# An RWKV layer in fp32 on one core: reordered last steps, and idle matmuls in TensorE's first waits

## The chip, the cores and the metric

One Trainium2 chip, one NeuronCore. The metric is the device time of one execution in microseconds (us). TensorE (PE) multiplies, VectorE (DVE), ScalarE (ACT) and GpSimd (POOL) do the elementwise work, and SyncE (SP) issues the transfers.

## The reference

An RWKV block over 32 sequences of 128 tokens and 512 channels, all in fp32. Cut to its steps:

```python
xn = ln(x); sx = token_shift(xn, prev1)
xxx = tanh((xn + sx*maa_x) @ maa_w1)                 # five small mixtures
x5 = xn + sx * (maa_stack + xxx @ maa_w2)
w = exp(-exp(time_decay + tanh(x5[1] @ decay_w1) @ decay_w2))
k, v, r, g = x5[0] @ Wk.T, x5[2] @ Wv.T, x5[3] @ Wr.T, silu(x5[4] @ Wg.T)
# per head of 16 channels, over the tokens t:
#   out_t = r_t @ (u * k_t v_t + s);  s = k_t v_t + w_t * s
att = groupnorm(out) * gn_w + gn_b
x = x + (att * g) @ Wo.T
xn2 = ln(x); xk, xr = mix(xn2, token_shift(xn2, prev0))
x = x + sigmoid(xr @ Wr2.T) * (square(relu(xk @ Wk2.T)) @ Wv2.T)
```

## The kernel before, in words

A block is two sequences (b = 0, 1) and there are 16 blocks. The program is unrolled into steps -2 to 17, and step i holds, as a software pipeline, the first half of block i + 1 or i + 2 (layer norm `xT`, `h`, the mixtures `mixW` to `mixV`, `z`, `decay`, then the dense products `k`, `g`, `r`, `v`), the recurrence of block i, and the second half of block i - 1 (group norm, `yT`, `wo`, layer norm, `x2T`, `kk`, `rr`, `wv`). The steps -2 to 0 lack the later parts and have little work. Step 15 (`LAST`) lacks the first half; in it the second half of block 14 runs with a recurrence of block 15, and the second half of block 15 is done one sequence at a time, by the functions `tail` (names with `@0` or `@1`). What is left of it lies in step 16.

The order of the work on each engine is written out by hand in lists: `PE_ORDER`, `ACT_ORDER`, `DVE_ORDER`, `POOL_ORDER` and `SP_ORDER` for the steps before the last, and `PE_LAST` and its likes (lines 75 to 91) for the last two. Each engine does its list in order and waits at semaphores inside each item.

The recurrence of a block has 8 units n = 0 to 7, one for each sequence and each group of 128 channels. The names that matter for it:

- `chain1`, `chain1b` (VectorE, from line 539): products of decays, k and r; the late half `chain1b` releases most of what follows. `rch1`, `rch1b` (GpSimd, from line 402) do the same for r, and `rch1b` stands behind `yT` in GpSimd's list of the last step.
- `M0` to `M7` (`mask`, SyncE, line 309): 8 copies of 12 KB each from `rst` to one of two buffers `rm`. Mn waits until `levels` of unit n - 2 is done (`levels_done`) and for GpSimd's `rchain` of its sequence.
- `A0` to `A7` (`levels`, TensorE, line 1020): 64 short products from such a buffer into `at_ps`. `E0` to `E7` (`evict`, ScalarE, line 863) take them out.
- `V0` to `V7` (`read_out`, TensorE, line 1081): two products with the first state `s0` and with `kvs`, then 16 short ones that wait for the eviction. The first state is loaded by `S0` and `S1` (`load_s0`, line 319), one buffer for both sequences, so `S1` waits for V3 (`read_done`).
- `kt0`, `kv0`, `kt1`, `kv1` (`turn_k`, `outer`): the state between the two halves of a sequence; `aT0`, `aT1` (`turn_att`): turns the result of a sequence.

For the second half: `yT` on TensorE turns `cen` (line 1127, 8 transposes) when GpSimd's `gn_scale` (line 484) is done. ScalarE's `yT` (line 848) takes the result out, GpSimd's `yT` (line 489) multiplies it with the gate, and then `wo.0` and `wo.1` can start (line 1119, 8 instructions each). For sequence 0 of the last block the chain aT0, `att0`, `gn_sum@0`, `gn_sub@0`, `gn_square@0`, `gn_var@0`, `gn_std@0`, `gn_rec@0`, `gn_scale@0` leads to `yT@0`.

At the start TensorE waits for four small loads (`sel_in`, with `ident` among them) and for `setup`, which counts the memsets of GpSimd and VectorE. SyncE's list of step 0 has M1 and S0 behind M0 and the load of `x`. `columns` (line 1111) does the dense products: 32 instructions for a group such as `k`.

A matmul in fp32 is two instructions in the trace, a transpose is one.

Of the kernel before, what the change touches and what calls it, by code (L numbers as in the profile page):

```python
# [71 lines left out]
LAST = NBLK - 1  # L72
POST = ("gn_sum", "gn_sub", "gn_square", "gn_var", "gn_std", "gn_rec", "gn_scale", "yT", "wo", "ln2_stats",
        "ln2", "x2T", "kk", "rr", "wv")
PE_LAST = {LAST: ["kt0", "V7", "kv0", "wv.0", "aT1", "A0", "wv.1", "V0", "A1", "c02_1", "V1", "c1v_1", "A2", "V2",
                  "A3", "V3", "yT", "kt1", "wo.0", "kv1", "wo.1", "aT0", "A4", "V4", "yT@0", "A5", "V5", "x2T", "A6", "V6",
                  "wo@0", "A7", "V7+", "kk.0", "aT1+", "kk.1", "x2T@0", "rr.0", "rr.1", "kk@0", "yT@1", "rr@0"],
           LAST + 1: ["wv.0", "wo@1", "wv.1", "wv@0", "x2T@1", "kk@1", "rr@1", "wv@1"]}
ACT_LAST = {LAST: ["kt0", "dec0", "att1", "E0", "gn_square", "gn_std", "E1", "vtm1", "E2", "E3", "yT", "kt1", "dec1",
                   "att0", "E4", "gn_square@0", "gn_std@0", "E5", "yT@0", "x2T", "E6", "E7", "att1+", "kk",  # L80
                   "gn_square@1", "x2T@0", "gn_std@1", "rr", "kk@0", "yT@1", "rr@0"],
            LAST + 1: ["x2T@1", "kk@1", "rr@1"]}
# [4 lines left out]
POOL_LAST = {LAST: ["gn_sub", "rch1", "wv", "c02_1", "gn_scale", "bon1", "yT", "rch1b", "gn_sub@0", "gn_scale@0",  # L87
                    "ln2_stats", "yT@0", "ln2_stats@0", "gn_sub@1", "gn_scale@1", "yT@1"],
             LAST + 1: ["ln2_stats@1", "wv"]}
SP_LAST = {LAST: ["M1", "S0", "F1", "M2", "out", "x2", "x2@0", "x2@1", "M3", "M4", "M5", "S1", "M6", "M7"],  # L90
           LAST + 1: ["out", "out@0", "out@1"]}


class Block:
# [21 lines left out]
def build(nc, A):  # L116
    ctx = ExitStack()
    with ctx:
        def sb(name, shape, dt=F32):
            return ctx.enter_context(nc.sbuf_tensor(name, shape, dt))  # L120
# [11 lines left out]
        dec1 = sb("dec1", [P, G, DEC])  # L132
        vecs = sb("vecs", [P, 16, G])
        ident = sb("ident", [P, P])
# [47 lines left out]
        yT = sb("yT", [P, G, TB])  # L182
        sq = yT[:, :, :].rearrange("p g t -> p (g t)")
        prev0 = sb("prev0", [P, G, NB])
        x2 = sb("x2", [P, NB, E])
# [17 lines left out]
        att_ps = ctx.enter_context(nc.psum_tensor("att_ps", [P, 2, NB, G, 64], F32))  # L203
# [49 lines left out]
        def ran(name, step):  # L253
            blk = step + AHEAD[name]
            return 0 <= blk < NBLK and not (blk == LAST and name in POST)
# [27 lines left out]
        def units(step):  # L283
            return step >= 0 and step < NBLK
# [11 lines left out]
        def _(sp):  # L296
# [35 lines left out]
            def step(i, at_):  # L332
                for name in SP_LAST.get(i, SP_ORDER if i < LAST else []):
                    if "@" in name:
# [502 lines left out]
        def _(ac):  # L837
# [163 lines left out]
            def step(i, at_):  # L1001
                for name in ACT_LAST.get(i, ACT_ORDER if i < LAST else []):
                    if "@" in name:
                        tail(name[:-2], int(name[-1]))
                    elif name == "att1+":
                        stage("att1", i + 1, at_.plus(1))
                    elif name[0] == "E":
                        if units(i):
                            evict(at_, int(name[1:]))
                    elif ran(name, i):  # L1010
                        stage(name, i, at_)
# [4 lines left out]
        def _(pe):  # L1016
# [33 lines left out]
            def turn_k(at_, b):  # L1050

                pe.wait_ge(kchain, at_.count(2 * NK, NK * (b + 1)))
                if at_.past(2, b - 1):
                    pe.wait_ge(att_ready, at_.count(2, b - 1))
                if at_.past(2, b):
                    pe.wait_ge(kvs_ready, at_.count(2, b))
                for g in range(G):
                    last = pe.transpose(kv_ps[:, g * P:(g + 1) * P], k64[:, 64 * g:64 * g + P], ident[:, :])
                last.then_inc(kt_done, 1)

            def outer(at_, b):

                pe.wait_ge(kt_ready, at_.count(2, b + 1))
                pe.wait_ge(vtm_ready, at_.count(2, b + 1))
                for g in range(G):
                    v = bass.AP(vtm[b], g * 2 * P, [[2 * E, 64], [64, G], [48, 2], [1, S]])
                    last = pe.matmul(kv_ps[:, g * P:(g + 1) * P], kt[:, g * P:(g + 1) * P], v,  # L1067
                                     start=True, stop=True)
                last.then_inc(kv_done, 1)

            def turn_att(at_, b):

                pe.wait_ge(attT_ready, at_.count(2, b + 1))
                pe.wait_ge(kvs_ready, min(at_.count(2, b + 2), 2 * NBLK))
                if at_.past(2, b):
                    pe.wait_ge(att_ready, at_.count(2, b))
                for g in range(G):
                    last = pe.transpose(kv_ps[:, g * P:(g + 1) * P], bonv[:, b, g, :], ident[:, :])
                last.then_inc(aT_done, 1)

            def read_out(at_, n):

                b, g = n // G, n % G
                o = att_ps[:, :, b, g, :]
                if g == 0:
                    pe.wait_ge(kvs_ready, at_.count(2, b + 1))
                    pe.wait_ge(s0_in, at_.count(32, 16 * (b + 1)))
                    pe.wait_ge(rchain, at_.count(2 * NR, NR * (b + 1)))
                    if at_.past(2, b - 1):
                        pe.wait_ge(attT_ready, at_.count(2, b - 1))  # L1090
                pe.matmul(o[:, 0, :], s0[:, g, :], rst[:, b, g, R64A:RST], start=(g == 0), stop=False,
                          skip_group_check=True)
                pe.matmul(o[:, 1, :], kvs[b][:, g * P:(g + 1) * P], rst[:, b, g, R64B:R16C], start=(g == 0),
                          stop=False, skip_group_check=True)
                pe.wait_ge(at_ready, at_.count(UNITS, n + 1))
                for odd in range(2):
                    for quad in range(4):
                        h = 2 * quad + odd
                        first = (g * HG + h) * 32
                        for c in range(2):  # L1100
                            rows_ = slice(64 * c, 64 * c + 64)
                            last = pe.matmul(o[32 * quad:32 * quad + 32, c, :],  # L1102
                                             vtm[b][rows_, first:first + 32], at[rows_, h, :], start=False,
                                             stop=(g == G - 1), skip_group_check=True)
                last.then_inc(read_done, 1)
# [161 lines left out]
            def step(i, at_):  # L1267
                for item in PE_LAST.get(i, PE_ORDER if i < LAST else []):
                    name, _, part = item.partition(".")
                    if "@" in name:  # L1270
                        tail(name[:-2], int(name[-1]))
                    elif name == "V7+":
                        read_out(at_, 7)
                    elif name == "aT1+":
                        turn_att(at_, 1)
                    elif name == "V7":
                        if units(i - 1):
                            read_out(at_.plus(-1), 7)
                    elif name in ("kt0", "kt1"):
                        if units(i):  # L1280
                            turn_k(at_, int(name[2:]))
                    elif name in ("kv0", "kv1"):
                        if units(i):
                            outer(at_, int(name[2:]))
                    elif name in ("aT0", "aT1"):
                        if ran(name, i):
                            turn_att(at_.plus(AHEAD[name]), int(name[2:]))
                    elif name[0] == "A":
                        if units(i):
                            levels(at_, int(name[1:]))  # L1290
                    elif name[0] == "V":
                        if units(i):
                            read_out(at_, int(name[1:]))
                    elif ran(name, i):
                        stage(name, i, at_, int(part or 0))
            run(step)


# [43 lines left out]
```

## Time and profile before

| | us |
|---|---|
| median of 3 runs | 1679.78 |
| the three runs | 1679.78, 2635.2, 1679.77 |
| the profiled execution | 1679.46 |
| its span, first to last instruction | 1677.7 |
| TensorE busy (matmul) | 1572.8 (94%) |
| VectorE, GpSimd, ScalarE busy | 997.1, 623.9, 512.8 |

Times in the profile count from the first instruction. "Idle before" is the time that an engine stood still in front of a group, and the arrow names what ended it; "issue" is time in which nothing that the profile shows was waited for. The granted clock is the share of TensorE's full 2.4 GHz: 1.00, or 0.50 for 1.2 GHz. For the first 23 us no clock was recorded and the windows say 1.00.

### The profile page before, as it was taken

The numbers are of one execution on the slowest core, as the hardware profiler recorded it, in microseconds if no ns is written. First come the engines' busy times: TensorE is split into PE (matmuls) and PEld (weight loads), VectorE is DVE, ScalarE is ACT, GpSimd is POOL, SyncE is SP. The second block draws the span as 40 slices with busy tenths as digits, with TensorE's granted clock in tenths as the row PEclk, the third lists the DMA queues.
The fourth block names the chain that finished last, engine by engine and source line by source line (L and its number), as shares of the span: only waits on it lengthen the run. The fifth ranks groups of instructions, "written<-read, shape, count | busy, mean of one in ns | idle before, by whom it ended". The sixth has DMA issues, their size and how long they took to land.

```text
span 1677.7 us, 45471 instructions
## 1 busy us (share of the span) xinstructions
PE 1572.8 (94%) x19680; PEld 1178.2 (70%) x19680; DVE 997.1 (59%) x1990; ACT 512.8 (31%) x910; POOL 623.9 (37%) x512
## 2 busy tenths in 40 slices
PE   4869799999999999999999999999999999999788
PEld 3658577777767777776777777677777767777454
DVE  3255665767566566756656675665667666555442
ACT  1122333324232332423233232322323232232231
POOL 3133442525244253524325352432535243252311
PEclk8879899999999999999999999999999999999799
DMA  7010100102010010201001020201102020010200
GB/s 272 0 34 25 47 23 21 51 18 63 22 59 24 21 61 7 64 22 61 22 23 61 6 64 21 61 22 34 49 7 64 21 61 22 22 47 8 61 16 25
DMA packets 56423, 67.70 MB, mean 40 GB/s; under 512 B 23264, under 2 KB 40032, under 8 KB 55200
## 3 DMA queue, kind: packets, MB, share of 16 engines
q1 hardware_dynamic: 56224, 64.79, 12.3%
q8 instruction: 156, 2.56, 0.7%
q14 instruction: 43, 0.35, 0.1%
HBM read 43.75 MB, written 8.39 MB: 31 GB/s over the span
## 4 chain that ended last, share of the span: by engine, by line
PE 77%; DVE 13%; ACT 4%; POOL 2%; issue 2%; SPq 1%; DMA 1%; ACTq 0%; POOLq 0%; DVEq 0%
PE pair L1111 27%; PE pair L1119 19%; PE pair L1165 4%; PE at_ps L1045 4%; PE at_ps L1038 3%; PE pair L1189 2%; PE kv_ps L1067 2%; PE att_ps L1102 2%; DVE kT L585 2%; PE pair L1127 2%; DVE x L674 2%; PE pair L1191 2%; PE pair L1145 2%; POOL cen L477 2%; DVE gT L704 1%
## 5 line engine op out<-in xcount | busy, mean ns | idle before, releaser
L1111 PE MATMUL pair<-x,wts 128*128 128x256 f32 x2048 | 463.5, 385 | 16.5 <-ACT kT L859 15.2
L1111 PEld LDWEIGHTS pair<-x,wts 128*128 128x128 f32 x2048 | 386.9, 191 | 80.1 <-ACT kT L859 18.0
L451 POOL TENSOR_TENSOR x<-x,xnT 128x1024 f32<-128x1024 f32 x80 | 178.5, 2231 | 226.8 <-DVE x L674 226.1
L674 DVE SCALAR_TENSOR_TENSOR x<-pair,vecs,sx 128x256 f32<-128x256 f32 x320 | 132.4, 475 | 123.8 <-PE pair L1165 123.4
L868 ACT ACTIVATE at<-at_ps 128x512 f32<-128x512 f32 x128 | 76.2, 596 | 194.9 <-PE at_ps L1045 194.7
L1119 PE MATMUL pair<-wts,yT 128*128 128x512 f32 x240 | 112.3, 612 | 4.1 <-POOL yT L489 4.1
L1045 PE MATMUL at_ps<-rm,kc 128*16 128x128 f32 (+1 forms) x2048 | 112.5, 279 | 0.0
L1119 PE MATMUL pair<-wts,cen 128*128 128x512 f32 x240 | 110.8, 604 | 0.0
L1111 PE MATMUL pair<-yT,wts 128*128 128x256 f32 x480 | 107.8, 382 | 0.0
L1119 PE MATMUL pair<-wts,sx 128*128 128x512 f32 x240 | 107.0, 599 | 0.7 <-ACT cen L854 0.7
L1038 PEld LDWEIGHTS at_ps<-rm,kc 128*8 128x8 f32 (+5 forms) x6144 | 67.4, 97 | 49.0 <-issue 37.5
L1111 PEld LDWEIGHTS pair<-yT,wts 128*128 128x128 f32 x480 | 89.9, 190 | 14.4 <-issue 2.8
L1038 PE MATMUL at_ps<-rm,kc 128*8 128x32 f32 (+5 forms) x6144 | 83.7, 197 | 10.5 <-DMA rm<-rst 9.7
L462 POOL TENSOR_TENSOR bonv<-bonv,p 128x256 f32<-128x256 f32 x32 | 43.3, 1352 | 130.7 <-DVE p L690 130.7
L555 DVE SCALAR_TENSOR_TENSOR bonv<-rT,vecs,kT 128x128 f32<-128x128 f32 x128 | 36.5, 347 | 92.8 <-ACT rT L859 62.0
L1165 PE MATMUL pair<-h,maa 32*128 32x128 f32 x1024 | 78.1, 293 | 10.9 <-DVE gT L704 7.4
L472 POOL TENSOR_TENSOR bonv<-bonv,p 128x256 f32<-128x256 f32 x32 | 24.5, 767 | 170.0 <-DVE p L697 170.0
L1165 PEld LDWEIGHTS pair<-h,maa 32*128 32x128 f32 x1024 | 65.4, 194 | 22.8 <-DVE gT L704 11.9
L1119 PEld LDWEIGHTS pair<-wts,sx 128*128 128x128 f32 x240 | 44.4, 190 | 52.4 <-issue 50.2
L408 POOL TENSOR_TENSOR rT<-rT,t 128x256 f32<-128x256 f32 x32 | 36.8, 1148 | 117.6 <-DVE p L568 117.6
L1119 PEld LDWEIGHTS pair<-wts,yT 128*128 128x128 f32 x240 | 44.3, 194 | 50.8 <-issue 49.0
L1045 PEld LDWEIGHTS at_ps<-rm,kc 128*16 128x16 f32 (+1 forms) x2048 | 78.4, 105 | 0.6
(192 smaller groups left out, 2679.6 us busy)
## 6 DMA issues: line engine op xcount, KB each, us to landing
rm<-rst SPq DMA_DIRECT2D x1024, 12.0 KB, 1.8
xu<-in_x SPq DMA_DIRECT2D x16, 512.0 KB, 3.9
wts<-in_wts SPq DMA_DIRECT2D x8, 1024.0 KB, 14.1
kvs<-in_s SPq DMA_DIRECT2D x32, 256.0 KB, 3.0
s<-in_s SPq DMA_DIRECT2D x32, 256.0 KB, 2.9
x<-in_x SPq DMA_DIRECT2D x15, 512.0 KB, 4.8
out<-sx SPq DMA_DIRECT2D x15, 512.0 KB, 3.0
prev<-in_prev SPq DMA_DIRECT2D x32, 4.0 KB, 3.5
```

The source lines that it names most:

```text
L408: gp.tensor_tensor(leaf[:, :, 2:4], leaf[:, :, 2:4], t2[:, :].rearrange("p (f q) -> p f q", q=2)[:, :, 0:1] .broadcast_to([P, G * 32, 2]), ...
L451: gp.tensor_tensor(t, t, xnT[:, :, :, 1:L1].rearrange("p g b t -> p (g b) t"), ALU.add).then_inc(x5_ready, 1)
L462: gp.tensor_tensor(leaf[:, :, 2:4], leaf[:, :, 2:4], m2[:, :, :, 0], ALU.add)\
L477: gp.tensor_tensor(cen[:, :, :].rearrange("p b (h d) -> p (b h) d", d=S), axn[:, 0:NB * E].rearrange("p (h d) -> p h d", d=S), gsum[:, :]. ...
L555: last = ve.scalar_tensor_tensor(bonv[:, b, g, :], rb[:, g, :], vecs[:, FAAAA, g:g + 1], kb[:, g, :], ALU.mult, ALU.mult)
L674: last = ve.scalar_tensor_tensor(seqs(x5[q], g), ps[:, :, g * L:(g + 1) * L], vecs[:, vec, g:g + 1], seqs(sx, g), ALU.add, ALU.mult)
L868: ac.activation(at[:, :, :], at_ps[:, :].rearrange("p (h t) -> p h t", h=HG), ACT.Copy)\
L1038: pe.matmul(out[32 * quad:32 * quad + m, :, col:col + 4], kc4[b][:, g, hi - m:hi], rm[p][:, :, cr:cr + 4], start=True, stop=True)
L1045: last = pe.matmul(out[64 * c + lo:64 * c + lo + m, :, 16 * s:16 * s + 16], kc16[b][:, g, first:first + m], rm[p][:, :, cr:cr + 16], start ...
L1111: last = pe.matmul(ps[:, g // 2, TB * (g % 2):TB * (g % 2 + 1)], wts[:, m, k, g * P:(g + 1) * P], source[:, k, :], start=(k == 0), stop=(k ...
L1119: last = pe.matmul(ps[:, b, :], source[:, k, b * L:(b + 1) * L], wts[:, m, k, :], start=(k == 0), stop=(k == G - 1))
L1165: last = pe.matmul(ps[:, b, g * L:(g + 1) * L], rows_[lo:lo + MAA, g * P:(g + 1) * P], src, start=True, stop=True)
```

## The change

In `PE_LAST[LAST]` the turn `yT` moves from behind V3 to in front of A3. In `ACT_LAST[LAST]` `yT` moves ahead of the eviction E3. In `SP_LAST[LAST]` the copies `M3` move ahead of `out`, `x2`, `x2@0` and `x2@1`, and `S1` moves ahead of `M4` and `M5`. And TensorE does idle matmuls in the steps -2 to 0: `IDLE` says how many stand ahead of which item, in front of all of its waits. Each multiplies `ident` (128 by 128) by `ident` into a part of `att_ps` that nobody reads before V0 of step 0 overwrites it. There are 155 of them.

```diff
 PE_LAST = {LAST: ["kt0", "V7", "kv0", "wv.0", "aT1", "A0", "wv.1", "V0", "A1", "c02_1", "V1", "c1v_1", "A2", "V2",
-                  "A3", "V3", "yT", "kt1", "wo.0", "kv1", "wo.1", "aT0", "A4", "V4", "yT@0", "A5", "V5", "x2T", "A6", "V6",
+                  "yT", "A3", "V3", "kt1", "wo.0", "kv1", "wo.1", "aT0", "A4", "V4", "yT@0", "A5", "V5", "x2T", "A6", "V6",
...
-ACT_LAST = {LAST: ["kt0", "dec0", "att1", "E0", "gn_square", "gn_std", "E1", "vtm1", "E2", "E3", "yT", "kt1", "dec1",
+ACT_LAST = {LAST: ["kt0", "dec0", "att1", "E0", "gn_square", "gn_std", "E1", "vtm1", "E2", "yT", "E3", "kt1", "dec1",
...
-SP_LAST = {LAST: ["M1", "S0", "F1", "M2", "out", "x2", "x2@0", "x2@1", "M3", "M4", "M5", "S1", "M6", "M7"],
+SP_LAST = {LAST: ["M1", "S0", "F1", "M2", "M3", "out", "x2", "x2@0", "x2@1", "S1", "M4", "M5", "M6", "M7"],
            LAST + 1: ["out", "out@0", "out@1"]}
+
+
+IDLE = {(-2, "xT"): 14, (-2, "h"): 27, (-1, "mixW"): 3, (-1, "z"): 17, (-1, "mixG"): 6, (-1, "k.0"): 3, (-1, "g.0"): 4,
+        (-1, "mixR"): 10, (-1, "mixV"): 6, (-1, "r.0"): 4, (-1, "v.0"): 4, (-1, "c1v_0"): 5, (-1, "h"): 12, (0, "mixW"): 3,
+        (0, "kt0"): 5, (0, "A0"): 14, (0, "V0"): 18}
...
             def step(i, at_):
                 for item in PE_LAST.get(i, PE_ORDER if i < LAST else []):
                     name, _, part = item.partition(".")
+                    for _ in range(IDLE.get((i, item), 0)):
+                        pe.matmul(att_ps[:, 0, 0, 0:2, :].rearrange("p g t -> p (g t)"), ident[:, :], ident[:, :],
+                                  start=True, stop=True)
```

## Rows read from the trace of the kernel before

**Rows 1.** The page: granted clock in 40 slices; two groups (busy, mean ns | idle).

```profile
PEclk8879899999999999999999999999999999999799
...
L451 POOL TENSOR_TENSOR x<-x,xnT 128x1024 f32<-128x1024 f32 x80 | 178.5, 2231 | 226.8 <-DVE x L674 226.1
L674 DVE SCALAR_TENSOR_TENSOR x<-pair,vecs,sx 128x256 f32<-128x256 f32 x320 | 132.4, 475 | 123.8 <-PE pair L1165 123.4
```

**Rows 2.** Windows of TensorE: length, busy (count), granted clock, DMA share, GB/s.

```profile
29.90:43.60 13.70, 11.25 (x72) 0.50 0.25 100
...
207.40:1560.00 1352.60, 1330.70 (x17007) 1.00 0.12 35
```

**Rows 3.** Timeline of TensorE, first steps: start, length, engine, line, operands [idle before].

```profile
11.43 1.94 PE L1127 MATMUL pair<-ident,xu 128*128 128x128 f32 x8 [11.43 <-DVE xu L641]
19.95 3.54 PE L1145 MATMUL pair<-xu,maa 128*128 128x128 f32 x16 [6.58 <-DVE xu L666]
...
30.59 1.97 PE L1171 MATMUL pair<-x,dec 128*64 128x128 f32 x16 [4.09 <-POOL x L451]
...
40.35 8.74 PE L1111 MATMUL pair<-x,wts 128*128 128x256 f32 x32
...
65.16 9.97 PE L1111 MATMUL pair<-x,wts 128*128 128x256 f32 x32 [0.26 <-POOL x L451]
76.24 7.17 PE L1111 MATMUL pair<-x,wts 128*128 128x256 f32 x32 [1.11 <-ACT rT L859]
...
92.10 3.78 PE L1145 MATMUL pair<-xu,maa 128*128 128x128 f32 x16 [3.08 <-DVE p L697]
...
177.78 2.05 PE L1145 MATMUL pair<-xu,maa 128*128 128x128 f32 x16 [2.30 <-DVE p L697]
```

**Rows 4.** Timeline of all engines, first steps: what starts beside TensorE.

```profile
5.90 0.96 POOL L393 MEMSET vtm<- 128x1024 f32 x1
...
98.61 5.00 SPq L316 DMA_DIRECT2D rm<-rst  x8
...
110.15 0.58 SPq L323 DMA_DIRECT2D s<-in_s  x1
...
113.07 0.66 PE L1091 MATMUL att_ps<-rst,s 128*128 128x64 f32 x2 [4.32 <-issue]
...
122.29 1.16 PE L1165 MATMUL pair<-hg,maag 32*128 32x128 f32 x16
```

**Rows 5.** Timeline of SyncE's queue (SPq), last step.

```profile
1559.81 5.99 SPq L316 DMA_DIRECT2D rm<-rst  x8
...
1571.29 29.17 SPq L316 DMA_DIRECT2D rm<-rst  x24
```

**Rows 6.** Timeline of GpSimd (POOL), last step.

```profile
1568.87 1.98 POOL L484 TENSOR_TENSOR cen<-cen,gsum 128x1024 f32<-128x1024 f32 x1
...
1585.14 2.34 POOL L489 TENSOR_TENSOR yT<-yT,gT 128x1024 f32<-128x1024 f32 x1 [13.42 <-ACT yT L848]
```

**Rows 7.** Timeline of TensorE, last step.

```profile
1562.99 0.83 PE L1045 MATMUL at_ps<-rm,kc 128*16 128x128 f32 x15
...
1577.44 0.82 PE L1038 MATMUL at_ps<-rm,kc 128*4 128x32 f32 x48 [7.31 <-DMA rm<-rst]
...
1581.13 1.97 PE L1127 MATMUL pair<-ident,cen 128*128 128x128 f32 x8
...
1587.63 6.45 PE L1119 MATMUL pair<-wts,yT 128*128 128x512 f32 x8 [4.09 <-POOL yT L489]
...
1595.09 3.70 PE L1119 MATMUL pair<-wts,yT 128*128 128x512 f32 x8
1598.63 0.60 PE L1078 MATMUL kv_ps<-ident,bonv 128*128 128x128 f32 x4
...
1604.04 0.66 PE L1091 MATMUL att_ps<-rst,s 128*128 128x64 f32 x2 [3.65 <-issue]
...
1605.66 1.11 PE L1237 MATMUL pair<-ident,x 128*128 128x128 f32 x4
```

## The prediction, made blind

> **What bounds the kernel now.** I read the page first: the granted clock in 40 slices shows nines nearly everywhere and lower digits only in the first five slices and the last two [rows 1]. Next the windows of TensorE: from 207 to 1560 us it is busy for 1330.7 of 1352.6 us at full clock [rows 2]. Nothing in the diff touches those steps except that they start earlier or later, so the middle is a constant. What is left is the ramp (0 to 126 us, steps -2 to 0) and the last step with its tail (from 1559 us). In a window of the ramp, 29.9 to 43.6 us, TensorE works 11.25 us of 13.7 and has a granted clock of 0.50, the 1.2 GHz level [rows 2]. The timeline of TensorE then shows what that costs and who releases it: groups of 16 or 32 instructions separated by gaps that end on VectorE, ScalarE or GpSimd [rows 3, 4]. For the last step I read the timelines of three engines side by side [rows 5 to 7]: TensorE stands 7.31 us for the third mask, 4.09 us for GpSimd's gate, and 3.65 us for the first state of the second sequence.
>
> The profiled execution is 1679.46 us (span 1677.7 and 1.8 around it). The median of the three runs is 1679.78, so I work from 1679.46.
>
> **Part 1: idle matmuls, the unit price.** One idle matmul is 128 rows by 128 columns in fp32, and the trace has such products as two instructions each. The nearest rows are line 1145: 16 instructions in 2.05 us at full clock and 3.54 us at half [rows 3], that is 0.25 us and 0.44 us for one idle matmul. I take 0.25 once the clock is up. No group waits for anything, so each costs nothing while its time fits in the gap in front of it, and its excess otherwise.
>
> Start: TensorE also waits for `setup`, whose last writer is the memset that ends at 6.86 [rows 4]; the first transposes start at 11.43. In those 4.5 us lie 14 idle matmuls: 3.5 us if all are fast, 6.2 if all are slow, so the edit costs 0 to 1.7. The transposes behind them (8 in 1.94 us, slow) would run in about half that time, a gain of 0 to 0.9. I take zero for the two together.
>
> Before `h`: 27 x 0.25 = 6.75 against a gap of 6.58 [rows 3], an excess of 0.2. The 16 instructions of line 1145 go from 3.54 to 2.05, so 1.5 less. Net -1.3. Before `z`: 17 x 0.25 = 4.25 against 4.09, +0.2.
>
> From `z` (30.59) to `k` (40.35) 9.8 us pass. Behind `z` the order is mixK on TensorE, 4 operations of VectorE (1.9 us in all), one of GpSimd (2.2 us) [rows 1]; `z` takes 1.97 us slow [rows 3], and I halve it and mixK's equally long group (16 narrow instructions take 1.16 at full clock [rows 4]). That gives 1.1 + 1.2 + 1.9 + 2.2 = 6.4 plus hand-overs. Beside it TensorE does mixG and decay, and the 3 idle matmuls of `k.0` (0.75 us): I take 7.0, so -2.8. `k` itself goes from 8.74 to the 7.17 that the same 32 instructions take in `v` [rows 3]: -1.6.
>
> The 4 idle matmuls ahead of `v.0` are 1.0 in a gap of 1.11 [rows 3], free; those of `g.0` stand in front of the same kind of wait, ScalarE's eviction of the group before. Those of `mixW`, `mixG`, `mixR`, `mixV` and `c1v_0` (28) stand at gaps that end on VectorE or ScalarE in the same way; I count no excess for them, and put 0.5 us of it in the bounds. `r` starts at 65.16, and `v` at 76.24, 11.1 later; at full clock that is 7.0 of pitch and 1.1 of gap, so -2.9 [rows 3]. `r` now has a gap of only 0.26, since mixV in front of it is slow; with mixV fast the gap opens to about 1 us, which the 4 idle matmuls fill, and the two leave some -0.2.
>
> The `h` of step -1 (92.10) is slow too, 3.78 against 2.05, behind 12 idle matmuls in 3.08 us. I count **nothing** for it: the first mask copies leave at 98.61 [rows 4], released by GpSimd behind VectorE's long chain, and this starts after `c1v_0`, whose time doesn't depend on `h`. The masks, and in SyncE's queue behind them the first state (issued 110.15), set when V0 can start at 113.07. So 3 + 5 + 14 + 18 idle matmuls of step 0 stand on cover that stays: 18 x 0.25 = 4.5 before V0, where the gap is 4.32 and grows by what A0 and `z` gain. If that cover were gone, the 40 would cost 10 us.
>
> From V0 (113.07) to mixG (122.29) lie 9.2 us of work, nearly all at half clock [rows 4]. Halved it would be 4.6; the short instructions don't halve, and I take 5.4: -3.8. VectorE's chain behind mixG releases the later groups, so the gain is kept, and the saturated middle [rows 2] only passes it on.
>
> Ramp: -1.3 + 0.2 - 2.8 - 1.6 - 0.2 - 2.9 - 3.8 = **-12.4 us**. Bounds: if every window stayed as it is and all groups only fit, 0; if start and transposes also give their 0.9 and V0 to mixG its 4.6, -14.
>
> **Part 2: the last step.** On SyncE's queue the copies of M2 end at 1565.8; then come out, x2, x2@0, x2@1, and M3 to M5 begin at 1571.29 [rows 5]. Eight copies take 4.9 us of issue, and A3 starts at 1577.44, so 6.1 after M3's first issue. M3 ahead of `out` starts at 1565.8 (its buffer is free once A1 is done, at 1563.8 [rows 7]), and A3 is released at 1571.9. The four other transfers start 4.9 us later; their first reader works after 1590.
>
> What is late next is `yT`. gn_scale ends at 1570.85 [rows 6]. The transposes now run first: 1570.95 to 1572.0 at full clock. From the start of the transposes (1581.13, slow) to GpSimd's start (1585.14) 4.0 us pass [rows 6, 7], so 3.1 with fast ones: GpSimd gates from 1574.1 to 1576.5 (2.34 us). A3, then V3 (whose eviction E3 now stands behind ScalarE's `yT`, about 1 us later than it could be) and kt1 lie in the same time and end near 1576. `wo.0` starts at **1576.7 instead of 1587.63**: 10.9 earlier.
>
> From `wo.0` to aT0 11.0 us pass, with `wo.0` at 6.45 (half clock) where `wo.1` takes 3.70 [rows 7]. The stretch in front of it still has gaps near 1 us and only short work, so I leave it slow: aT0 at 1587.7. M4: rch1b on GpSimd is behind its `yT` and moves with it. M5's copies end at 1571.29 + 29.17 = 1600.46 [rows 5], so M4's began two times 5.0 us before, at 1590.5; 11 us earlier is 1579.5, and they land some 6.1 us later at 1585.6, before aT0. S1, ahead of M4, waits for V3 (done near 1575.4) and is issued while M4 would wait for rch1b anyway: it costs M4 nothing, and V4's 3.65 us go [rows 7]. In their place comes the norm of sequence 0: from aT0 (1598.63) to yT@0 (1605.66) 7.0 us, of which at most half a us was slack. yT@0 starts at 1587.7 + 6.6 = 1594.2, after a new idle time of some 3 us on TensorE: 11.4 earlier. M6 and M7 are released by A4 and A5 and move along; behind this all is the same order and TensorE's work.
>
> Tail: **-12 us** (11.4 and a few tenths from queue time). Bounds: if the clock stays up in `wo.0`, 2.7 more, -14.5. If M3's copies or VectorE's chain beside GpSimd's `yT` lose 4 to 6 us, -6.
>
> A rule speaks to the slow `wo.0`. The 8 transposes at 11.43 take 1.94 us, slow, and the clock is not up behind them [rows 3]; the trace can't say if work of that kind would lift it. The Trainium skill (TensorE: Matmul & The Clock Gate, Part 4: PE-mode transpose) says that transposes don't count as busy time for the clock gate. By it the moved turn fills the gap in time only, and the tail is -12; if they do count, it is -14.5. It changes no other term, as the idle operations of the diff are matmuls and not transposes.
>
> **Sum.** 1679.5 - 12.4 - 12 = **1655 us**.
>
> **The rivals.**
> (a) *The ramp is bound by its chains.* The gaps end on VectorE, ScalarE and GpSimd, and groups that run faster may only make longer gaps; the clock's phase may also differ. For it: `h` at 92.10, which I count at zero for this reason. Against it: `k` and `r` are long groups with their release at their own end. Worth -5 instead of -12.4: 1662.5.
> (b) *A new wait takes the tail's place.* M4's copies, rch1b or VectorE's chain hold A4 or kt1; 12 becomes 6: 1661.
> (c) *All is fast*: the ramp gives 14, the tail 14.5, and the slow stretch of the next step's start (which has no idle matmuls) shortens by chance by 3: 1648.
> (d) *The idle matmuls don't lift the clock, and cost.* They multiply an identity, mostly zeros. At 0.44 us each, the groups of 14, 27, 17, 12 and 18 take 6.2, 11.9, 7.5, 5.3 and 7.9 in gaps of 4.5, 6.58, 4.09, 3.08 and 4.32: 16.2 over for 88 of them, 28 for all 155. With the tail 28 - 12 = +16: **1696**, slower than before. It decides against the change once more than 12 / 28 of the idle time is slow and nothing behind it gets faster. Against it: after 3.54 us of line 1145, of the same shape, the next products are fast.
> (e) *The change doesn't do what it says*: the order on TensorE is fixed by hand and the groups can't go missing; M3 may find its buffer busy, but A1 is done at 1563.8. I give it nothing beyond (b).
>
> **How the numbers follow.** Forecast 0.60, (a) 0.15, (b) 0.11, (c) 0.09, (d) 0.05. The forecast's own spread is 4 us each way (bounds of the two parts). The range 1646 to 1667 holds it, (a), (b) and (c), and leaves out (d) and some of each edge. Two per cent is about what a measurement of this kernel can tell from no change. Faster by more is below 1646.2 us, just beyond (c): half of (c) and a small part of the forecast's edge, 0.09. Over 2% slower is above 1713: past (d), 0.01. Within 2%: 0.90.
>
> **What would show it.** Right: granted clock 1.00 from about 20 to 126 us, `k` and `r` at 7.2 us, V0 released near 104; GpSimd's gate near 1576 less the ramp's gain; no wait of V4 for the state, and some 3 us idle before yT@0. Wrong: idle groups of over 0.3 us each; `z` or `h` late behind them; a wait of A4 for its mask; a middle that changes length.

## The result, and the profile after

The changed kernel takes 1659.41 us (median of 4 runs, 1657.67 to 1660.9) against 1679.78 (4 runs). One of the four runs of before, 2635.2 us, was disturbed; the comparison leaves it out. The ratio is 0.9882, with a 95% interval of 0.9863 to 0.9902: 20 us less, inside two per cent. The profiled execution after took 1657.67 us (span 1655.9), the fastest of the four, so stage by stage I compare 1655.9 with 1677.7, 21.8 us. Measured again beside later experiments, the same kernel came out 17.2 us below the one before (e12 below), so the profile shown here is of a favourable execution.

The granted clock on the page, to lay beside [rows 1]:

```profile
PEclk9999799999999999999999999999999999999999
```

The low digits of the ramp are gone but for one slice, the fifth, which neither kernel fills with idle matmuls. TensorE's timeline of the first steps after (start, length, engine, line, operands, idle before), answering to [rows 3, 4]; line 1276 is the idle matmul, and the lines between the lists and it have moved by 5:

```profile
7.00 6.15 PE L1276 MATMUL att_ps<-ident 128*128 128x128 f32 x28 [7.00 <-POOL vtm L398]
12.99 1.04 PE L1132 MATMUL pair<-ident,xu 128*128 128x128 f32 x8
13.86 6.19 PE L1276 MATMUL att_ps<-ident 128*128 128x128 f32 x54
20.60 2.05 PE L1150 MATMUL pair<-xu,maa 128*128 128x128 f32 x16 [0.55 <-DVE xu L671]
...
29.77 1.09 PE L1176 MATMUL pair<-x,dec 128*64 128x128 f32 x16
...
36.67 7.14 PE L1116 MATMUL pair<-x,wts 128*128 128x256 f32 x32
...
59.73 7.14 PE L1116 MATMUL pair<-x,wts 128*128 128x256 f32 x32
...
67.99 7.17 PE L1116 MATMUL pair<-x,wts 128*128 128x256 f32 x32 [0.22 <-ACT rT L864]
...
83.87 2.05 PE L1150 MATMUL pair<-xu,maa 128*128 128x128 f32 x16 [0.41 <-DVE p L702]
...
105.93 0.41 PE L1096 MATMUL att_ps<-rst,s 128*128 128x64 f32 x2 [2.09 <-issue]
...
107.96 1.66 PE L1194 MATMUL pair<-bonv,headall 128*128 128x512 f32 x2
109.42 1.91 PE L1196 MATMUL pair<-p,headall 128*128 128x512 f32 x2
...
112.61 1.16 PE L1170 MATMUL pair<-hg,maag 32*128 32x128 f32 x16
```

28 idle instructions take 6.15 us in the first group, part of it slow, and 54 take 6.19 in the second: 0.23 us for one idle matmul at full clock. The first group overruns its gap, so the transposes start at 12.99 and not at 11.43; they then take 1.04 us instead of 1.94, and `h` starts 0.65 us later than before. From there each stage up to `v` is shorter. `k` takes 7.14 us where it took 8.74, and from the start of `r` to the start of `v` 8.3 us pass where it was 11.1. Two rows go against the forecast: V0 waits until 105.93, and the two products with `headall` (107.96 and 109.42) take 1.66 and 1.91 us, slow again in part. Ahead of V0 the idle matmuls end 2.1 us too early; that this gap is what lets the clock fall is tested in e7.

SyncE's queue beside it, answering to the two transfer rows of [rows 4]:

```profile
90.38 5.65 SPq L321 DMA_DIRECT2D rm<-rst  x8
...
102.99 0.58 SPq L328 DMA_DIRECT2D s<-in_s  x1
```

The last step after: SyncE's queue, then GpSimd's gate, then TensorE with the rest of the tail, answering to [rows 5 to 7].

```profile
1550.86 11.06 SPq L321 DMA_DIRECT2D rm<-rst  x16
...
1571.12 19.69 SPq L321 DMA_DIRECT2D rm<-rst  x29
```

```profile
1565.77 2.36 POOL L494 TENSOR_TENSOR yT<-yT,gT 128x1024 f32<-128x1024 f32 x1 [2.97 <-ACT yT L853]
```

```profile
1562.12 1.60 PE L1132 MATMUL pair<-ident,cen 128*128 128x128 f32 x8 [1.27 <-POOL cen L489]
1564.41 0.82 PE L1043 MATMUL at_ps<-rm,kc 128*4 128x32 f32 x48 [0.69 <-DMA rm<-rst]
...
1568.28 3.67 PE L1124 MATMUL pair<-wts,yT 128*128 128x512 f32 x8 [0.25 <-POOL yT L494]
...
1572.96 3.70 PE L1124 MATMUL pair<-wts,yT 128*128 128x512 f32 x8
1576.50 0.60 PE L1083 MATMUL kv_ps<-ident,bonv 128*128 128x128 f32 x4
...
1578.47 0.43 PE L1096 MATMUL att_ps<-rst,s 128*128 128x64 f32 x2
...
1583.12 1.12 PE L1242 MATMUL pair<-ident,x 128*128 128x128 f32 x4 [3.43 <-POOL x L514]
...
1591.43 3.70 PE L1247 MATMUL pair<-wts,xu 128*128 128x512 f32 x8
...
1638.41 6.68 PE L1258 MATMUL att_ps<-xu,wts 128*128 128x128 f32 x32 [3.57 <-DVE xu L816]
```

M2 and M3 are now one group of 16 copies, and the wait of A3 for its mask went from 7.31 us to 0.69. The turn `yT` stands in front of it, `wo.0` waits 0.25 us for the gate instead of 4.09, and V4 at 1578.47 waits for nothing. In their place TensorE stands 3.43 us for the norm of sequence 0, as forecast. What was not forecast is the 3.67 us of `wo.0`, at full clock.

In a table, with the prediction's steps (us, after minus before; the last row adds up only to rounding):

| stretch | predicted | profile |
|---|---|---|
| start to `h` | +0.2 | +0.65 |
| `h` to `z` | -1.3 | -1.5 |
| `z` to `k` | -2.8 | -2.9 |
| `k` to the end of its eviction | -1.6 | -1.6 |
| to `r`, and `r` to `v` | -0.2, -2.9 | -0.1, -2.8 |
| `v` to V0 of step 0 | 0 | +1.1 |
| V0 to mixG | -3.8 | -2.5 |
| ramp | -12.4 | -9.7 |
| the middle, to V2 of the last step | 0 | +0.4 |
| V2 to `wo.0` | -10.9 | -10.1 |
| `wo.0` to aT0 | 0 | -2.8 |
| aT0 to wo@0 | -0.5 and some tenths | -0.9 |
| the rest (`kk@1` slower at 1638.41) | 0 | +1.2 |
| all | -24.4 | -21.8 |

### The profile page after: what moved, and what is told of

The parts are those of the page before. It is cut to its first block, busy times and chain, and to the rows that moved or that the text cites. A ratio compares the mean times of both kernels' runs of the same rounds, so it can differ in the third digit from the quotient of the medians.

```text
span 1655.9 us, 46091 instructions
## 1 busy us (share of the span) xinstructions
PE 1590.0 (96%) x19990; PEld 1200.0 (72%) x19990; DVE 997.2 (60%) x1990; ACT 513.0 (31%) x910; POOL 624.3 (38%) x512
## 3 DMA queue, kind: packets, MB, share of 16 engines
q8 instruction: 158, 2.59, 0.6%
## 4 chain that ended last, share of the span: by engine, by line
PE 78%; DVE 14%; ACT 4%; POOL 2%; issue 2%; SPq 0%; DMA 0%; ACTq 0%; POOLq 0%; DVEq 0%
PE pair L1116 28%; PE pair L1124 19%; PE pair L1170 4%; PE at_ps L1050 4%; PE at_ps L1043 3%; PE pair L1194 2%; PE kv_ps L1072 2%; DVE kT L590 2%; PE att_ps L1107 2%; PE pair L1132 2%; PE pair L1196 2%; DVE x L679 2%; POOL cen L482 2%; PE pair L1150 2%; DVE gT L709 1%
## 5 line engine op out<-in xcount | busy, mean ns | idle before, releaser
L1124 PEld LDWEIGHTS pair<-wts,cen 128*128 128x128 f32 x240 | 43.3, 189 | 48.5 <-issue 46.8
```

The lines of the kernel that those rows point to most:

```text
L1124: last = pe.matmul(ps[:, b, :], source[:, k, b * L:(b + 1) * L], wts[:, m, k, :], start=(k == 0), stop=(k == G - 1))
```

## The experiments

There are twelve experiments. Four take the change apart (e1, e2, e4, e5), four take up single claims (e3, e6, e7, e10), and the last four build on what was found, with the changed kernel itself measured again among them. The kernel before was measured beside each, at 1678.4 to 1678.7 us, and the ratios are to that.

**e1_order_only.** The three lists of the last step alone. This diff, and the others where nothing else is said, is against the changed kernel.

```diff
-IDLE = {(-2, "xT"): 14, ...
+IDLE = {}
```

> The changed kernel without its 155 idle matmuls: the three lists of the last step alone. Theory (two independent gains): the ramp is that of the kernel before, the last step gives what it gave in the changed kernel, 13.7 us, so 1666 us, and wo.0 starts some 10 us earlier than before relative to the end of V2. Rival (the tail's gain was partly a matter of where the clock's changes fell, wo.0 being fast by chance): wo.0 takes near 6.4 us again and the kernel is at 1669.

1668.42 us, ratio 0.9942 (0.9927 to 0.9956): 10 us less. This is half of the change's gain, but 13.7 us were expected. The rival is the nearer one: it said 1669 us and a slow `wo.0`, and `wo.0` takes 5.45 us here. What neither theory has is a wait in front of it. Its rows on TensorE, VectorE and GpSimd:

```profile
1577.37 1.12 PE L1061 MATMUL kv_ps<-ident,k 128*128 128x128 f32 x4 [3.52 <-DVE k L632]
1578.28 5.45 PE L1122 MATMUL pair<-wts,yT 128*128 128x512 f32 x8
```

```profile
1573.00 2.55 DVE L619 TENSOR_TENSOR kc<-kc,cu 128x256 f32<-128x256 f32 x1
```

```profile
1572.92 2.34 POOL L492 TENSOR_TENSOR yT<-yT,gT 128x1024 f32<-128x1024 f32 x1 [2.36 <-ACT yT L851]
```

kt1 waits 3.52 us for the end of VectorE's late chain. In that chain the product of line 619 takes 2.55 us, and in the changed kernel's profile (there line 621) 0.42. It starts 0.08 us behind GpSimd's gate, an operation of 2.34 us. So wo.0, in the list behind kt1, comes 3 us after its gate is ready (1575.26), and runs slow.

**e2_idle_only.** The idle matmuls with the old last step.

```diff
-SP_LAST = {LAST: ["M1", "S0", "F1", "M2", "M3", "out", "x2", "x2@0", "x2@1", "S1", "M4", "M5", "M6", "M7"],
+SP_LAST = {LAST: ["M1", "S0", "F1", "M2", "out", "x2", "x2@0", "x2@1", "M3", "M4", "M5", "S1", "M6", "M7"],
...
-                  "yT", "A3", "V3", "kt1", "wo.0",
+                  "A3", "V3", "yT", "kt1", "wo.0",
...
-"vtm1", "E2", "yT", "E3", "kt1", "dec1",
+"vtm1", "E2", "E3", "yT", "kt1", "dec1",
```

> The kernel before with the idle matmuls and with its own order of the last step. Theory: k starts near 36.7, mixG of step 0 near 112.6, 9 to 10 us earlier than before, the last step as before: 1670 us. Rival (the idle matmuls also change the clock later in the kernel, in the steps that have none): more or less than that by 2 us or more, with the difference behind 130 us.

1669.23 us, ratio 0.9946 (0.9931 to 0.9961), with `k` and mixG where the theory had them:

```profile
36.26 7.14 PE L1116 MATMUL pair<-x,wts 128*128 128x256 f32 x32
...
112.31 1.16 PE L1170 MATMUL pair<-hg,maag 32*128 32x128 f32 x16
```

The gain is the 9 to 10 us of the theory. The two halves give 10.3 and 9.5 us, together 19.8, and the whole gave 20.4 and, measured again, 17.2: within the scatter of the runs they add.

**e4_copies_only and e5_turn_only.** One half of the new order each, against the kernel before: SyncE's list in e4,

```diff
-SP_LAST = {LAST: ["M1", "S0", "F1", "M2", "out", "x2", "x2@0", "x2@1", "M3", "M4", "M5", "S1", "M6", "M7"],
+SP_LAST = {LAST: ["M1", "S0", "F1", "M2", "M3", "out", "x2", "x2@0", "x2@1", "S1", "M4", "M5", "M6", "M7"],
```

and `yT` on TensorE and ScalarE in e5:

```diff
-                  "A3", "V3", "yT", "kt1", "wo.0",
+                  "yT", "A3", "V3", "kt1", "wo.0",
...
-"vtm1", "E2", "E3", "yT", "kt1", "dec1",
+"vtm1", "E2", "yT", "E3", "kt1", "dec1",
```

> The kernel before with SyncE's new list for the last step alone (M3 ahead of the output and the loads, S1 ahead of M4). Theory (two waits in series, each edit takes away its own): A3 comes 5 us earlier, the turn yT stays behind V3, so GpSimd's gate and wo.0 come 5 to 6 us earlier: about 1673 us. Rival (the copies alone do it, the turn was hidden): all 13 us, 1666.

> The kernel before with yT ahead of A3 and of E3 alone, SyncE's list as before. Theory (two waits in series): A3 stays at its wait for M3, GpSimd's gate is done early, and wo.0 starts as soon as A3, V3 and kt1 are done, some 6 us earlier than before; rch1b is early too, and V4 waits for the first state behind M5: 5 to 8 us, near 1673. Rival (the copies are the whole wait): within 2 us of the kernel before.

1672.2 us (0.9968, 0.9957 to 0.9979) and 1671.03 us (0.9957, 0.9942 to 0.9972). TensorE's rows for A3 and wo.0 in the first and in the second:

```profile
1571.86 0.82 PE L1041 MATMUL at_ps<-rm,kc 128*4 128x32 f32 x48 [2.39 <-DMA rm<-rst]
...
1581.01 5.37 PE L1122 MATMUL pair<-wts,yT 128*128 128x512 f32 x8 [4.10 <-POOL yT L492]
```

```profile
1577.62 0.82 PE L1041 MATMUL at_ps<-rm,kc 128*4 128x32 f32 x48 [5.49 <-DMA rm<-rst]
...
1582.21 5.68 PE L1122 MATMUL pair<-wts,yT 128*128 128x512 f32 x8
```

With the copies alone A3's wait is 2.39 us, and GpSimd's gate is the wait that is left (4.10). With the turn alone the gate has gone and A3's 5.49 us are left. Each alone gives 6.5 or 7.7 us and both together 10.3, so the two don't add. Most of the missing 3.9 us lies ahead of wo.0: counted from the start of V2, wo.0 comes 6.0 us earlier in e4, 5.5 in e5, and only 8.4 with both (e1). The long operation of e1 is in e5 too (line 619 takes 2.56 us there), but hidden behind A3's wait; it comes to the surface when both waits are gone. Both rivals, one edit doing all of it, fall.

**e3_idle_turns.** The test of the rule that the prediction had weighed.

```diff
-                        pe.matmul(att_ps[:, 0, 0, 0:2, :]..., ident[:, :], ident[:, :], start=True, stop=True)
+                        for _ in range(2):
+                            pe.transpose(att_ps[:, 0, 0, 0:2, :]..., ident[:, :], ident[:, :])
```

> The changed kernel with each idle matmul replaced by two transposes of the identity into the same place (one instruction each, so as many instructions of the same shape). Theory A (transposes don't count for the clock, the rule that the prediction weighed): the clock stays at half through the idle groups, a transpose takes 0.24 us, the 310 of them overrun their gaps, and the kernel is near 1690 us or slower. Theory B (they count like matmuls): the granted clock of the first 100 us is near 1.00 as in the changed kernel and the time within 3 us of it, 1657 to 1662.

1658.83 us (2 runs), ratio 0.9881 (0.9861 to 0.9901). The window of the ramp (length, busy, granted clock, DMA share, GB/s) and the first two idle groups:

```profile
24.00:107.80 83.80, 76.58 (x676) 1.00 0.16 60
```

```profile
7.00 5.94 PE L1277 MATMUL att_ps<-ident 128*128 128x128 f32 x28 [7.00 <-POOL vtm L398]
...
13.64 6.06 PE L1277 MATMUL att_ps<-ident 128*128 128x128 f32 x54
```

Theory A falls and B stands: transposes lift and hold TensorE's clock as matmuls do. The lifting is seen in the durations, since no clock is recorded that early: up to 19.7 us this kernel's TensorE does nothing but transposes, 28 idle ones and the 8 of `xT`, and the 54 that follow take 6.06 us, full speed. The holding is the granted clock of 1.00 from 24 to 108 us.

**e6_state_back.** S1 behind M4 and M5 again.

```diff
-... "x2@1", "S1", "M4", "M5", "M6", "M7"],
+... "x2@1", "M4", "M5", "S1", "M6", "M7"],
```

> The changed kernel with S1 back behind M4 and M5. Theory (the first state's wait is a part of the gain of its own): S1 is issued near 1581 and lands 3.5 us later, V4 waits for it, and yT@0 starts some 3 us later than in the changed kernel: 1662 us. Rival (the norm of sequence 0, which ends the wait before yT@0, hides the load whole): within 1 us of the changed kernel, 1659.

1659.52 us, the changed kernel's time.

```profile
1585.38 0.66 PE L1096 MATMUL att_ps<-rst,s 128*128 128x64 f32 x2 [2.42 <-issue]
...
1587.81 1.11 PE L1242 MATMUL pair<-ident,x 128*128 128x128 f32 x4 [0.73 <-POOL x L514]
```

V4 waits 2.42 us for the state again, and yT@0 only 0.73 us for GpSimd, 6.6 us behind aT0 as in the changed kernel. The rival holds: the norm hides the load, and moving S1 gave nothing. (The prediction had named the norm as what comes in place of this wait, and counted no gain for it.)

**e7_start9_v27.** Two groups of another size.

```diff
-IDLE = {(-2, "xT"): 14, ... (0, "V0"): 18}
+IDLE = {(-2, "xT"): 9, ... (0, "V0"): 27}
```

> The changed kernel with 9 instead of 14 idle matmuls ahead of the first transposes and 27 instead of 18 ahead of V0 of step 0. Theory (the first group overruns its gap by 1.6 us and the V0 group leaves 2.1 us idle, in which the clock falls): first transposes near 11.5 instead of 12.99, no half clock near 108 to 111 us, mixG of step 0 2 to 3 us earlier: 1656.5 us. Rival (the clock is up earlier with 14, and h pays with 9 what the start gains): h starts at 20.6 again and only the V0 group gives 1 us: 1658.5.

1656.18 us, ratio 0.9866 (0.9849 to 0.9882).

```profile
10.97 1.21 PE L1132 MATMUL pair<-ident,xu 128*128 128x128 f32 x8
...
18.76 2.05 PE L1150 MATMUL pair<-xu,maa 128*128 128x128 f32 x16 [0.55 <-DVE xu L671]
```

```profile
98.16 6.29 PE L1276 MATMUL att_ps<-ident 128*128 128x128 f32 x54
104.29 0.33 PE L1096 MATMUL att_ps<-rst,s 128*128 128x64 f32 x2
...
109.33 1.16 PE L1170 MATMUL pair<-hg,maag 32*128 32x128 f32 x16
```

The transposes start 2.0 us earlier and `h` 1.8 us earlier than in the profile above, and `h` is as fast, so five fewer idle matmuls cost nothing of the clock. (Single executions differ here: over all profiles `h` starts at 19.9 to 20.6 us with 14 idle matmuls in the first group, at 18.8 to 19.2 with 9, and at 19.8 to 20.1 with none.) V0 follows the longer group at once, the clock stays up, and V0 to mixG takes 5.0 us (6.7 changed, 9.2 before). Both claims of the theory hold: 3.3 us earlier at mixG.

**e10_kt1_behind.** kt1 no longer ahead of wo.0.

```diff
-"A3", "V3", "kt1", "wo.0", "kv1", "wo.1", "aT0", "A4", "V4",
+"A3", "V3", "wo.0", "kt1", "wo.1", "kv1", "A4", "aT0", "V4",
```

> The changed kernel with TensorE's list of the last step changed to wo.0, kt1, wo.1, kv1, A4, aT0, V4: kt1 no longer stands ahead of wo.0. Theory (VectorE's chain, when it meets GpSimd's gate, ends 3 us late and holds kt1 and with it wo.0, in some executions): wo.0 starts with the gate in every execution, the runs lie closer together, and the median is 1 to 2 us below the changed kernel, 1657.5. Rival (kv1 and aT0 come later and the norm of sequence 0 behind them decides): same or up to 1.5 us slower.

1658.7 us (1658.18 to 1660.74), ratio 0.9883 (0.9868 to 0.9897). In its profile wo.0 starts with the gate and takes 3.67 us, but aT0 comes 10.2 us behind it instead of 8.2, for kv1 and A4 are now between. What one place gives the other takes. The time can't tell the two apart; the profile speaks for the rival. VectorE's chain is held up here as well, at its last operation, a copy of 64 elements a partition, in the first row. The second row is the same operation in the changed kernel's profile:

```profile
1565.16 2.35 DVE L634 COPY k<-kT 128x64 f32<-128x64 f32 x1
```

```profile
1565.70 0.19 DVE L634 COPY k<-kT 128x64 f32<-128x64 f32 x1
```

In e10 it started 0.13 us behind the gate, in the changed kernel's profile 0.07 us ahead of it.

**e11_wo_first, e9_tail_fills, e8_more_fills, e12_changed_again.** These were measured side by side. e11 has the groups of e7 and a milder order:

```diff
-"A3", "V3", "kt1", "wo.0", "kv1", "wo.1", "aT0", "A4", "V4",
+"A3", "V3", "wo.0", "kt1", "kv1", "wo.1", "aT0", "A4", "V4",
```

e9 adds to e11 idle matmuls in the last step:

```diff
+IDLE_TAIL = {(LAST, "yT"): 4, (LAST, "A3"): 3, (LAST, "wo.0"): 3, (LAST, "yT@0"): 14}
...
+                    for _ in range(IDLE_TAIL.get((i, item), 0)):
+                        if _ == 0:
+                            pe.wait_ge(m2_ready, 2 * NBLK)
+                        pe.matmul(bank_t(0, 1)[:, 0:P], ident[:, :], ident[:, :], start=True, stop=True)
```

e8 has all of e9 and two groups more:

```diff
-        (0, "kt0"): 5, (0, "A0"): 14, (0, "V0"): 27}
+        (0, "kt0"): 5, (0, "A0"): 14, (0, "V0"): 27, (1, "V0"): 21}
...
+                    for _ in range(14 if (i, item) == (LAST + 1, "kk@1") else 0):
+                        pe.matmul(bank_t(1, 1)[:, 0:P], ident[:, :], ident[:, :], start=True, stop=True)
```

> The kernel with 9 and 27 idle matmuls (e7_start9_v27) and the order wo.0, kt1, kv1, wo.1, aT0, A4, V4. Theory (in most executions VectorE's chain meets GpSimd's gate, ends late, and kt1 holds wo.0 by 2 to 3 us; A4 ahead of aT0 was what cost e10_kt1_behind its gain): wo.0 starts 0.1 us behind the gate, aT0 8.9 us later, median 1.5 us below e7_start9_v27, 1654.7. Rival (kv1 now waits for ScalarE's eviction of kt1 and wo.0 runs at half clock just as long): within 0.7 us of it.

> e11_wo_first with idle matmuls in the last step too: 4 ahead of yT, 3 ahead of A3, 3 ahead of wo.0 and 14 ahead of yT@0, into the half of the bank that wo@0 fills later. Theory (the gaps of the last step let the clock fall as those of the ramp do): no half clock from 1550 to 1600 us, wo.0 takes 3.7 us, 2 to 3 us below e11_wo_first, 1652. Rival (most of what runs slow there waits for something else anyway, and the idle matmuls delay A3 and V3): within 1 us.

> e9_tail_fills with two more groups: 21 idle matmuls ahead of V0 of step 1 (5.4 us of gap in the changed kernel) and 14 ahead of kk@1 (3.6 us). Theory (each gap costs what runs at half clock behind it): 3 us from step 1, 2 to 3 us from the end, 1647. Rival (the clock in step 1 falls in an earlier gap, which stays): only the end gives its 2 us, 1650.

> The changed kernel as it is, in the same job as the three above. Theory (its executions differ by whether VectorE's chain meets the gate): median 1659.5, spread 3 us, and in the profile kt1 waits for VectorE where the long operation of the chain takes over 2 us. Rival (one fixed time): all runs within 0.5 us.

| kernel | median | runs | ratio to before |
|---|---|---|---|
| e12, the changed kernel | 1661.13 | 1659.73 to 1661.62 | 0.9896 (0.9881 to 0.9911) |
| e11 | 1655.79 | 1653.37 to 1659.5 | 0.9867 (0.9851 to 0.9884) |
| e9 | 1653.83 | 1653.11 to 1657.55 | 0.9861 (0.9845 to 0.9878) |
| e8 | 1647.92 | 1647.68 to 1648.57 | 0.9819 (0.9804 to 0.9834) |

e12's profiled execution took 1661.62 us, 4 us more than the one shown above, with the same code. Its rows on TensorE and VectorE:

```profile
1570.00 1.12 PE L1063 MATMUL kv_ps<-ident,k 128*128 128x128 f32 x4 [2.59 <-DVE k L634]
1570.91 5.79 PE L1124 MATMUL pair<-wts,yT 128*128 128x512 f32 x8
```

```profile
1566.58 2.32 DVE L625 TENSOR_TENSOR du<-du,cu 128x8 f32<-128x8 f32 x1
```

Here the gate met the chain at another operation, line 625, eight elements wide, which takes 2.32 us instead of 0.17. kt1 waits 2.59 us, and wo.0 is slow, 5.79 against 3.67. At aT0 this execution is 4.8 us behind the first one: 1.3 from before V2's end, 1.4 since wo.0 starts later behind it, and 2.1 in wo.0. So what held the chain in e1 holds it in this kernel too; the profile shown first just escaped it. The theory of e12 holds, though the median is 1.6 us above it and the spread was 1.9 us and not 3.

Over all profiles: the chain and the gate overlap in eleven (all but before, e2 and e4). In ten of them one operation of the chain starts 0.05 to 0.13 us behind the gate and takes 2.3 to 2.6 us, whatever its size, and in the eleventh, the changed kernel's first profile, nothing of the chain starts in that time. That the gate is the cause is read from these coincidences; no run moves the gate by itself. Earlier in the chain the same is seen beside GpSimd's gn_scale in every profile, the kernel before included (2.15 us for line 585, which starts 0.11 us behind it), so there the change adds nothing.

e11 does not settle the order: its median is 0.4 us below e7's, its runs lie 6 us apart, and in its profile wo.0 is on time but takes 6.02 us, as its rival has it. e9 has a granted clock of 1.00 from 1550 to 1600 us and takes 3.67 us for wo.0, and the median is 2.0 lower, as expected, but the intervals overlap. e8's rows (wo.0, the end's idle group with `kk@1` behind it, and two windows):

```profile
1560.68 3.67 PE L1125 MATMUL pair<-wts,yT 128*128 128x512 f32 x8 [0.74 <-POOL yT L495]
```

```profile
1627.76 3.29 PE L1281 MATMUL att_ps<-ident 128*128 128x128 f32 x28
1631.49 3.84 PE L1259 MATMUL att_ps<-xu,wts 128*128 128x128 f32 x32 [0.44 <-DVE xu L817]
```

```profile
24.00:177.00 153.00, 140.24 (x1674) 1.00 0.12 41
1550.00:1640.00 90.00, 84.78 (x954) 1.00 0.11 36
```

With the clock at 1.00 nearly throughout, the kernel takes 1647.9 us and its four runs lie within 0.9 us. Compared with e12 that is 13 us less, and `kk@1` takes 3.84 us where it took 6.68. This is the fastest version; the theory had 1647. One half-clock stretch remains ahead of the last two microseconds, from about 178 to 181 us.

## Why the prediction was right, and where it was not

**The time** was 4.4 us above the forecast and within its range; the side is right, the size was forecast at 24 us and came out at 20 (17 when measured again), and it lies in "within two per cent". The mechanism is right in its two halves: e1 and e2 give 10.3 and 9.5 us where 12 and 12.4 were forecast. In the profile shown two errors of opposite sign nearly cancel: the ramp is 2.7 us short and `wo.0` 2.8 us better than forecast. That is luck, since `wo.0` is slow in most executions.

**The price of an idle matmul** was 0.25 us and measured 0.23. The slow price was 0.44 and measured 0.46 (the nine of e7's first group take 4.18 us). That the gaps swallow the groups is shown by the rows: in steps -2 and -1 up to 0.6 us of each filled gap is left but for the first group's, and 1.1 and 2.1 us ahead of A0 and V0. Rival (d), that they don't lift the clock, fell: 1.00 from 24 us on. Its counter-argument was weaker than it read: behind the 3.54 us of line 1145 the next products are fast, but behind the 3.78 us at 92.10 in the same trace they are not (16 products of line 1150 take 1.92 us there and 1.07 the first time). Rival (a), the chains eating the gain, had the ramp at -5 and fell with e2.

**The long stages** (`h`, `k`, `r`) came out within 0.2 us each. Each was a row at half clock set against a row of the same shape at full clock, and that is why they held. `z` to `k` came out as well (6.9 us for 7.0), but there 0.6 us of the 7.0 stood for hand-overs without a row. Two slips changed nothing: the groups of `mixW`, `mixG`, `mixR`, `mixV` and `c1v_0` have 30 idle matmuls in step -1, not 28, and the clock on the page before is low in slices 1, 2, 3, 5 and 38, not in five and the last two.

**The first group** failed a little: "I take zero for the two together" was +0.65 behind `h` in this profile, and some 0.4 on the average of those with the same group. The bound of 1.7 was the right reading, 1.56 us of it came, and e7 shows that it was avoidable.

**V0 to mixG** failed: -3.8 predicted, -2.5 measured. The step took full clock for the whole stretch, although the group before V0 ends 2.1 us short of it. The prediction says itself that this gap grows; from the end of `z` to V0 it was 6.3 us in the end, and 18 idle matmuls fill 4.2. With 27 the stretch gives 4.2 us (e7).

**`v` to V0** was to be unchanged and took 1.1 us more. The mask copies leave as long behind `h` as before (6.5 us), but from the first copy to S0 SyncE's queue needs 12.6 us instead of 11.54 [rows 4]. Over all profiles, `h` to V0 is 20.9 to 21.3 us in the four without idle groups and 22.0 to 22.7 in the ten with them. That the idle groups go with it is shown; why is open, since no run separates the copies' issue from the waits in that queue.

**The tail.** From V2 to `wo.0` the forecast held to 0.8 us in the first profile: both waits had to go, as e4 and e5 show, and rch1b and M4 followed. (A3 itself came 1.8 us later than forecast, at no cost, as the gate was done after it.) The norm is right as well: aT0 to yT@0 was forecast at 6.6 us and took 6.62. Two terms are off. "I leave it slow" for `wo.0` was too slow for the first profile (3.67 us), yet right in kind for most: of the ten profiles with both waits gone, it takes 3.67 us in four (the first one, e10, and the two with idle matmuls in the last step) and 4.7 to 6.0 in six. And VectorE's chain beside the gate, which the sum has at nothing (kt1 is to "end near 1576"; the chain stands only in the bounds and in rival (b)), is the term that makes the usual tail smaller: of the six profiles where kt1 stands ahead of `wo.0`, kt1 waits for VectorE in five, 0.6 to 3.5 us. So the mechanism of rival (b) was part of the usual case, at 0.6 to 3.5 us and not 6; the prediction had it apart. Behind the tail, `kk@1` at half clock took 6.68 us instead of 5.46, which the forecast left out; it takes 6.7 or 6.8 us in three profiles and 5.3 to 5.5 in the others, but for e8, where idle matmuls fill the gap ahead of it. The short ramp and the held chain together are why the median is above the forecast.

**A rule and the measurement.** The prediction weighed the sentence of the Trainium skill (TensorE: Matmul & The Clock Gate, Part 4: PE-mode transpose) that transposes don't count as busy for the clock. e3 decides against it for this fp32 case: 310 transposes in place of 155 matmuls, granted clock 1.00, the same time. So this rule doesn't explain the slow wo.0 of many executions; with the gaps of the last step filled (e9, e8) it takes 3.67 us. On the contention the Trainium skill (SBUF — State Buffer, the section "SBUF: two separate sides") says that of a GpSimd operation that reads SBUF and a VectorE operation with two SBUF inputs, the one that starts first keeps the other out for its whole instruction. The trace agrees: 0.42 us became 2.55, and 0.17 became 2.32, in both cases about the 2.35 us of the GpSimd operation that had started just before. In e10 and e11 it was a copy, with one input, that went from 0.19 to 2.35 us.

## What to carry to other kernels

Where an engine has a slow state after gaps, price a stage by setting its row in the slow state against a row of the same shape in the fast one; such terms held to 0.2 us here, while most terms that were put at zero missed, by 0.4 to 2.8 us. Size idle work by the gap as it will be after the change, since faster work in front widens it: a group that ends 2 us early gave back 1.6 of the 4.2 us that its stage had to give, and filling the last gaps brought the spread of the runs down with the time. Don't read a term off one execution: two profiles of the same changed kernel differ by 2.1 us in one group and by 2.6 in its start. When an operation moves earlier, look at what its engine shares with the one that it now meets.

## What the runs showed of the hardware

- Products of an identity with itself, mostly zeros, lift TensorE's clock from 1.2 to 2.4 GHz and hold it there, and so do transposes alone (e3): 28 instructions take 6.15 and 5.94 us, partly slow, the next 54 take 6.19 and 6.06, and the granted clock is 1.00 from 24 us on in both.
- For the first 23 us no clock is recorded and the windows say 1.00, while 8 transposes take 1.94 us, against 1.04 at full clock; durations tell it there.
- A VectorE operation of eight elements a partition took 2.32 us instead of 0.17 when it started 0.09 us behind a GpSimd operation of 2.37 us; one that started 0.07 us ahead of such an operation took its usual 0.19. Which operation of the chain is hit changes from run to run.
- With the clock up nearly throughout (e8), four runs lay within 0.9 us; the changed kernel's within 3.2, the kernel of e11 within 6.
